# Splitting the queries' first weight pieces inside the keys-and-values stage, reloading the first pair's tokens there, and storing keys and values by two tiles

## What is computed

```
xn = layernorm(x);  ctx = ctx_2048
q = rope(rms_norm((xn @ wq).reshape(B, L, 16, 128), q_norm_w))
k = rope(rms_norm((xn @ wk).reshape(B, L, 4, 128), k_norm_w)); v = xn @ wv
k_ctx = rms_norm((ctx @ wk_ctx).reshape(B, T, 4, 128), k_norm_w); v_ctx = ctx @ wv_ctx
x = x + tanh(g_xattn[0]) * attend(q, [k_ctx, k], [v_ctx, v]) @ wo
```

## Time and profile before

| | |
|---|---|
| time, median of 3 runs | 2215.08 us (2214.99 to 2220.88) |
| the profiled execution's own time | 2212.68 us |
| its span (first to last instruction) | 2210.9 us |
| TensorE (PE) busy | 1969.8 us, 89% |
| VectorE (DVE) busy | 1369.9 us, 62% |
| ScalarE (ACT) busy | 1074.2 us, 49% |
| GpSimd (POOL) busy | 426.6 us, 19% |
| mean granted TensorE clock | 0.963 of full speed |

### The profile page before, as it was taken

The page is one execution under the profiler, slowest core; times in us unless marked ns, Lnnn a source line. Parts: engine busy times, 40 slices in busy tenths (PEclk is TensorE's granted clock), DMA queues, the critical chain, the costliest instruction groups (busy, mean ns, idle before and its releaser), DMA issues. The chain is left out here.

```text
span 2210.9 us, 33071 instructions
## 1 busy us (share of the span) xinstructions
PE 1969.8 (89%) x10514; PEld 1493.7 (68%) x10514; DVE 1369.9 (62%) x2405; ACT 1074.2 (49%) x2590; POOL 426.6 (19%) x512
## 2 busy tenths in 40 slices
PE   6999479999999999997998999999979988886898
PEld 5888357777666767765786777787768865554454
DVE  6777366766666676764321765645555436885786
ACT  3333156665655666663111622112324417995998
POOL 1111034444434444440000000000000001222111
PEclk9999789999999999998999999999989999998999
DMA  5665762233223241105442412113257623331121
GB/s 216 247 247 218 264 177 81 75 88 89 74 78 87 77 103 41 30 20 191 165 149 72 148 58 69 51 51 95 85 192 260 210 84 104 99 112 49 49 58 43
DMA packets 194087, 254.58 MB, mean 115 GB/s; under 512 B 11782, under 2 KB 144022, under 8 KB 183580
## 3 DMA queue, kind: packets, MB, share of 16 engines
q1 hardware_dynamic: 193948, 252.87, 35.1%
HBM read 152.14 MB, written 100.68 MB: 114 GB/s over the span
## 5 line engine op out<-in xcount | busy, mean ns | idle before, releaser
L937 ACT ACTIVATE at_prob<-at_S,at_bias,at_rq 128x384 f32<-128x384 f32 (+1 forms) x256 | 184.3, 731 | 166.0 <-DVE at_bias L1023 159.8
L1034 DVE TENSOR_TENSOR at_pt_lo<-at_PT,at_pt_hi 128x512 fp32r<-128x512 f32 x224 | 148.9, 689 | 92.5 <-ACT at_pt_hi L944 92.3
L805 POOL TENSOR_SCALAR at_prob<-at_prob,at_rsum 128x384 f32<-128x384 f32 (+1 forms) x256 | 161.2, 643 | 176.4 <-DVE at_rsum L1029 176.3
L864 PE MATMUL at_PT<-c_ident,at_prob 128*128 128x128 f32 x896 | 127.7, 277 | 44.1 <-DVE at_pt_lo L1034 44.1
L1604 ACT ACTIVATE gu_silu<-gu_G 128x512 f32<-128x512 f32 x64 | 38.1, 597 | 244.1 <-PE gu_G L103 234.7
L944 ACT ACTIVATE at_pt_hi<-at_PT 128x512 fp32r<-128x512 f32 x224 | 127.9, 603 | 54.2 <-PE at_PT L864 54.2
L1014 DVE TENSOR_REDUCE at_nmax<-at_S 128x1 f32<-128x384 f32 (+1 forms) x256 | 147.9, 616 | 7.0 <-PE at_S L857 6.6
L864 PEld LDWEIGHTS at_PT<-c_ident,at_prob 128*128 128x128 f32 x896 | 98.0, 140 | 75.0 <-DVE at_pt_lo L1034 70.5
L1642 DVE TENSOR_TENSOR gu_h<-gu_silu,gu_U 128x512 f32<-128x512 f32 x64 | 43.9, 686 | 143.9 <-PE gu_U L103 96.9
L853 PE MATMUL at_S<-at_k_hi,at_q_hi 128*128 128x384 f32 (+1 forms) x256 | 114.0, 445 | 16.9 <-DVE at_q_lo L1039 13.5
L796 POOL TENSOR_TENSOR at_rq<-at_qv,c_minus_half 128x4 f32<-128x4 f32 x64 | 65.2, 1019 | 287.2 <-DVE at_qv L1009 287.2
(11 more groups left out here) (308 smaller groups left out, 5485.3 us busy)
## 6 DMA issues: line engine op xcount, KB each, us to landing
wide<-at_ot SPq DMA_DIRECT2D x64, 256.0 KB, 2.8
wide<-gu_h SPq DMA_DIRECT2D x64, 256.0 KB, 3.2
o_a<-wide SPq DMA_DIRECT2D x14, 1024.0 KB, 4.8
d_a<-wide SPq DMA_DIRECT2D x13, 1024.0 KB, 8.6
keys_hi<-kv_kt_hi SPq DMA_DIRECT2D x8, 1024.0 KB, 4.0
keys_lo<-kv_kt_lo SPq DMA_DIRECT2D x8, 1024.0 KB, 6.0
values_hi<-kv_v_hi SPq DMA_DIRECT2D x8, 1024.0 KB, 8.0
values_lo<-kv_v_lo SPq DMA_DIRECT2D x8, 1024.0 KB, 9.6
```

Source lines behind the costliest of these rows:

```text
L805: pool.tensor_scalar(prob[u % 2][:, h, 0:n], prob[u % 2][:, h, 0:n], rsum[:, s:s + 1], 1.0, ALU.mult, ALU.mult).then_inc(normed.sem, 1)
L864: last = pe.transpose(bank_of("p", u, kb)[:, h * P:(h + 1) * P], prob[u % 2][:, h, kb * P:(kb + 1) * P], c.ident[:])
L937: act.activation(prob[u % 2][:, h, 0:n], S[h][:, 0:n], ACT.Exp, bias=bias[:, s:s + 1], scale=rq[u % 4][:, h:h + 1], accum_out=sums[:, s:s ...
L1034: dve.tensor_tensor(pt_lo[f % 4][:], bank_of("p", u, kb)[:], pt_hi[f % 4][:].bitcast(F32), ALU.subtract).then_inc(pt_done.sem, 1)
```

## The change

A new function reserves tiles that outlive stage 1: two of stage 1's weight rooms (high and low parts of pieces 0 and 1, the context's weights) and its context tokens `t_hi[1]`, `t_lo[1]` are now the same memory as stage 2's first two query weight pieces and its tokens of pair 0.

- In the last turn of stage 1, SP loads query pieces 0 and 1 into x and cx after the token stores; after the stores at n = 4 it loads both sequences' tokens of pair 0 back from memory.
- Keys and values are stored after every two tiles (n = 2, 4, 6, 8), in transfers of 512 KB instead of 1 MB. A key row of such a transfer is 1 KB long, where the whole tile was contiguous before.
- After the last unit, ACT copies the high parts and DVE subtracts the low parts of the two pieces; PE runs 24 keep-awake products.
- Stage 2 no longer loads or splits pieces 0 and 1, nor loads the tokens of pair 0; PE's keep-awake goes, and its wait for the tables stands after the projections of units 0 and 1. SP issues the four table loads first and then raises the tokens' semaphores itself.

```diff
 def keys_values(nc, io, c, scr):
+        c.make_queries(nc)
...
-        w_hi = [mem.sb(f"w_hi{i}", [P, DC, 512], F32R) for i in range(4)]
-        w_lo = [mem.sb(f"w_lo{i}", [P, DC, 512], F32R) for i in range(4)]
+        w_hi = c.wq_hi + [mem.sb(f"w_hi{i}", [P, DC, 512], F32R) for i in range(2, 4)]
+        w_lo = c.wq_lo + [mem.sb(f"w_lo{i}", [P, DC, 512], F32R) for i in range(2, 4)]
...
-        t_hi = [mem.sb(f"t_hi{s}", [P, DC, TOK], F32R) for s in range(SRC)]
-        t_lo = [mem.sb(f"t_lo{s}", [P, DC, TOK], F32R) for s in range(SRC)]
+        t_hi = [mem.sb("t_hi0", [P, DC, TOK], F32R), c.xt_hi]
+        t_lo = [mem.sb("t_lo0", [P, DC, TOK], F32R), c.xt_lo]
...
-                for n in (TT, 2 * TT):
-                    s, _ = source(n - 1)
+                if not more:
+                    sp.wait_ge(*ln.xn_ready.at(turn, TT))
+                    for i in range(2):
+                        sp.dma_start((x, cx)[i][:], wq[:, :, i * 512:(i + 1) * 512]).then_inc(wq_arrived[i], 16)
+                for n in (2, 4, 6, 8):
+                    s, t = source(n - 1)
+                    tok, tiles = slice((t - 1) * P, (t + 1) * P), slice(t - 1, t + 1)
                     wait_apart(sp, kt_done, turn, n, passed)
-                    sp.dma_start(scr.k_hi[turn, s], kt_hi[s][:]).then_inc(kv_stored[s].sem, 16)
-                    sp.dma_start(scr.k_lo[turn, s], kt_lo[s][:]).then_inc(kv_stored[s].sem, 16)
+                    for dram, keys in ((scr.k_hi, kt_hi), (scr.k_lo, kt_lo)):
+                        sp.dma_start(dram[turn, s, :, :, tok], keys[s][:, :, tok]).then_inc(kv_stored[s].sem, 16)
                     wait_apart(sp, v_done, turn, n, passed)
...
+                    for dram, values in ((scr.v_hi, v_hi), (scr.v_lo, v_lo)):
+                        sp.dma_start(dram[turn, s, :, tiles, :],
+                                     values[s][:, tiles, :].bitcast(F32)).then_inc(kv_stored[s].sem, 16)
                     if more and n == TT:
                         store_context(turn + 1)
+                    if not more and n == TT:
+                        sp.wait_ge(*xt_stored.at(0, 32))
+                        sp.wait_ge(*V_full.at(turn, TT))
+                        sp.dma_start(c.xt_hi[:].bitcast(F32), scr.xt_hi[0]).then_inc(queries_arrived, 16)
+                        sp.dma_start(c.xt_lo[:].bitcast(F32), scr.xt_lo[0]).then_inc(queries_arrived, 16)
...
+            sp.wait_ge(queries_arrived, 2 * 16)
             for s in (xt_stored, ct_stored, *kv_stored):
...
             turns(pe, body)
+            keep_awake(pe, T[0], c, 2 * AWAKE)
...
             turns(act, body)
+            for i in range(2):
+                act.wait_ge(wq_arrived[i], 16)
+                act.wait_ge(*V_full.at(PAIRS - 1, TT))
+                act.activation(c.wq_hi[i][:], (x, cx)[i][:], ACT.Copy).then_inc(wq_hi_done, 1)
...
             turns(dve, body)
+            for i in range(2):
+                dve.wait_ge(wq_hi_done, i + 1)
+                dve.tensor_tensor(c.wq_lo[i][:], (x, cx)[i][:], c.wq_hi[i][:].bitcast(F32),
+                                  ALU.subtract).then_inc(wq_lo_done, 1)
...
 def attention(nc, io, c, scr):
+        AHEAD = 2
...
-            weights.load(sp, 0)
-            load_xt(0, 0)
             sp.dma_start(cosw[:], io["c_cos_tok"]).then_inc(setup, 16)
             sp.dma_start(sinw[:], io["c_sin_tok"]).then_inc(setup, 16)
             sp.dma_start(qw[:], io["L0_xattn_q_norm_w"].partition_broadcast(P)).then_inc(setup, 16)
             sp.dma_start(mask_f[:], io["c_diag_mask"]).then_inc(setup, 16)
-            weights.load(sp, 1)
+            for b in range(2):
+                sp.sem_inc(xt_arrived[b].sem, 32)
             load_kv(0, 0, 0)
-            for n in range(2, HKV):
+            for n in range(HKV - AHEAD):
                 weights.load(sp, n)
-                load_kv(0, 0, n - 1)
-            load_kv(0, 0, HKV - 1)
-            load_xt(0, 1)
...
-            pe.wait_ge(weights.arrived[0], 16)
-            keep_awake(pe, O, c, AWAKE)
-            pe.wait_ge(tables, 3)
...
-                    pe.wait_ge(weights.ready, g + 1)
+                    if g >= AHEAD:
+                        pe.wait_ge(weights.ready, g + 1 - AHEAD)
...
             project(0, 1, 1)
+            pe.wait_ge(tables, 3)
             chain(pe, step)
...
-            weights.split_hi(act, 0)
             square(0, 0)
             keep_queries(0, 0)
             square(0, 1)
-            for i in range(1, HKV):
+            for i in range(HKV - AHEAD):
                 weights.split_hi(act, i)
...
-            weights.split_lo(dve, 0)
             rotate(0, 0)
             split_queries(0, 0)
             rotate(0, 1)
-            for i in range(1, HKV):
+            for i in range(HKV - AHEAD):
                 weights.split_lo(dve, i)
             chain(dve, step)
...
+    def make_queries(self, nc):
...
+        self.wq_hi = [far(f"wq_hi{i}", [P, DC, 512]) for i in range(2)]
+        self.wq_lo = [far(f"wq_lo{i}", [P, DC, 512]) for i in range(2)]
+        self.xt_hi = far("xt_hi", [P, DC, TOK])
+        self.xt_lo = far("xt_lo", [P, DC, TOK])
```

More of the change, by code:

```diff
@@ L265, in keys_values @@
     with ExitStack() as ctx:
+        c.make_queries(nc)
         mem = Alloc(ctx, nc, "kv_")
         SRC = 2
-        w_hi = [mem.sb(f"w_hi{i}", [P, DC, 512], F32R) for i in range(4)]
-        w_lo = [mem.sb(f"w_lo{i}", [P, DC, 512], F32R) for i in range(4)]
+        w_hi = c.wq_hi + [mem.sb(f"w_hi{i}", [P, DC, 512], F32R) for i in range(2, 4)]
+        w_lo = c.wq_lo + [mem.sb(f"w_lo{i}", [P, DC, 512], F32R) for i in range(2, 4)]
         wk, wv = [2, 0], [3, 1]
+        wq = io["L0_xattn_wq"].rearrange("(k p) n -> p k n", p=P)
         names = ["L0_xattn_wk_ctx", "L0_xattn_wv_ctx", "L0_xattn_wk", "L0_xattn_wv"]
@@ L320, in keys_values @@
         xt_stored = mem.counter("xt_stored", 32)
-        kv_stored = [mem.counter(f"kv_stored{s}", 64) for s in range(SRC)]
+        kv_stored = [mem.counter(f"kv_stored{s}", 128) for s in range(SRC)]
+        wq_arrived = [mem.sem(f"wq_arrived{i}") for i in range(2)]
+        wq_hi_done = mem.sem("wq_hi_done")
+        wq_lo_done = mem.sem("wq_lo_done")
+        queries_arrived = mem.sem("queries_arrived")
         first_setup = mem.sem("first_setup")
@@ L606, in _ @@
             turns(dve, body)
+            for i in range(2):
+                dve.wait_ge(wq_hi_done, i + 1)
+                dve.tensor_tensor(c.wq_lo[i][:], (x, cx)[i][:], c.wq_hi[i][:].bitcast(F32),
+                                  ALU.subtract).then_inc(wq_lo_done, 1)
 def attention(nc, io, c, scr):
     with ExitStack() as ctx:
+        ctx.enter_context(c.queries)
         mem = Alloc(ctx, nc, "at_")
@@ L619, in attention @@
         S_N = UNITS * GROUP
-        wq_hi = mem.sb("wq_hi", [P, DC, HQ * HD], F32R)
-        wq_lo = mem.sb("wq_lo", [P, DC, HQ * HD], F32R)
+        AHEAD = 2
+        wq_hi = c.wq_hi + [mem.sb(f"wq_hi{g}", [P, DC, GW], F32R) for g in range(AHEAD, HKV)]
+        wq_lo = c.wq_lo + [mem.sb(f"wq_lo{g}", [P, DC, GW], F32R) for g in range(AHEAD, HKV)]
         wq = io["L0_xattn_wq"].rearrange("(k p) n -> p k n", p=P)
-        xt_hi = [mem.sb(f"xt_hi{b}", [P, DC, L], F32R) for b in range(2)]
-        xt_lo = [mem.sb(f"xt_lo{b}", [P, DC, L], F32R) for b in range(2)]
+        xt_hi = [c.xt_hi[:, :, b * L:(b + 1) * L] for b in range(2)]
+        xt_lo = [c.xt_lo[:, :, b * L:(b + 1) * L] for b in range(2)]
         k_hi = mem.sb("k_hi", [P, HKV, 2, 2, L], F32R)
@@ L642, in attention @@
         prob = [mem.sb(f"prob{i}", [P, GROUP, 2 * L]) for i in range(2)]
-        weights = WeightSplit(mem, [(wq[:, :, g * GW:(g + 1) * GW], whole, wq_hi[:, :, g * GW:(g + 1) * GW],
-                                     wq_lo[:, :, g * GW:(g + 1) * GW]) for g in range(HKV)], raw=prob)
+        weights = WeightSplit(mem, [(wq[:, :, g * GW:(g + 1) * GW], whole, wq_hi[g][:], wq_lo[g][:])
+                                    for g in range(AHEAD, HKV)], raw=prob)
         pt_hi = [mem.sb(f"pt_hi{i}", [P, GROUP * P], F32R) for i in range(4)]
@@ L738, in load_xt @@
                 own = slice(b * L, (b + 1) * L)
-                sp.dma_start(xt_hi[b][:].bitcast(F32), scr.xt_hi[turn, :, :, own]).then_inc(xt_arrived[b].sem, 16)
-                sp.dma_start(xt_lo[b][:].bitcast(F32), scr.xt_lo[turn, :, :, own]).then_inc(xt_arrived[b].sem, 16)
+                sp.dma_start(xt_hi[b].bitcast(F32), scr.xt_hi[turn, :, :, own]).then_inc(xt_arrived[b].sem, 16)
+                sp.dma_start(xt_lo[b].bitcast(F32), scr.xt_lo[turn, :, :, own]).then_inc(xt_arrived[b].sem, 16)
             def load_kv(turn, b, g):
@@ L756, in _ @@
             sp.dma_start(mask_f[:], io["c_diag_mask"]).then_inc(setup, 16)
-            weights.load(sp, 1)
+            for b in range(2):
+                sp.sem_inc(xt_arrived[b].sem, 32)
             load_kv(0, 0, 0)
-            for n in range(2, HKV):
+            for n in range(HKV - AHEAD):
                 weights.load(sp, n)
```

(28 more changed lines are left out.)

2 lines of the change are left out of this document (removed).

## The result

The changed kernel takes 2191.98 us (median of 4 runs, 2189.59 to 2192.94) against 2217.98 us before (4 runs, 2214.99 to 2222.79); the ratio is 0.9879, 95% interval 0.9856 to 0.9903. The forecast was 2192.8 us, in a range of 2188 to 2200. As a difference it was 22.3 us; the two profiled executions, 2212.68 and 2191.29 us, differ by 21.4.

The account below looks back on a forecast made before the run. PE, busy 89% of the span, was taken as the bound, with some 64 us of handover holding 23 us of PE work. Gains of 4.4 + 11.8 + 6.1 = 22.3 us from 2215.08 gave 2192.8 us, range 2188 to 2200.

Parts of the forecast that it names:

- drain of stage 1: End of stage 1: half the bytes left to store, so the barrier comes 4.4 us earlier; bounds 0 to 5.5.
- head of stage 2, from there to PE's first projection: Start of stage 2: PE's first projection 2.3 us after the first load's issue instead of 14.1; gain 11.8 us.
- the clock in units 0 and 1: First projection of stage 2: as slow as now, at 1.2 GHz, no gain; bounds 1.7 us gained to 0.9 lost.
- the other two pieces: Stage 2's weight splits: only two pieces left, both with free rooms, so 6.1 us go.
- the 5.4 allowed: Head of stage 2: the mask's load may take 5.4 us to land without cost; upper bound of cost 1.7 us.
- the 0.9 allowed: Bound of the clock term: 0.9 us lost if all 12 matmuls of the first projection are slow.
- The drain shrank: Opposite of a rival at stage 1's end: drain does not shrink, gain 17.9 us, 2197.2 us; chance 0.14.
- new wait: Rival at stage 2's head: tables, first keys or pieces 2 and 3 late; 16.2 us left, 2198.9; chance 0.10.
- the clock did not hold: Opposite of a rival: clock holds through the barrier, drain ends with DVE; gain 25.1 us, 2190.0; chance 0.08.
- swallowed: Rival later in stage 2: something waited for at its own time swallows the gain, 2215 us; chance 0.04.
- The choking queue: Rival in stage 1's turns: key stores in 1 KB rows choke the queue, ending 0.3% slower; chance 0.02.

Follow-up runs that it names:

- stores by four: The changed kernel, but keys and values stored once per source in transfers of 1 MB, as before; ratio 0.9929, median 2199.4 us.
- the stores alone: The kernel before with only one part of the change, keys and values stored by two tiles; ratio 0.9984.
- one piece ahead: The changed kernel, but only the first weight piece is split ahead, leaving three for stage 2; ratio 0.9938.
- tokens first: The changed kernel, but SP raises the tokens' semaphores ahead of the four table loads instead of behind them; ratio 0.9902.
- e10_after_beside: The changed kernel unaltered, on the same chip and in the same rounds as the run with the splits in the stands; ratio 0.9905.

## Why the prediction was right

The forecast's own terms and what they measured, in the profiled executions:

| term | predicted, us | measured, us | from |
|---|---|---|---|
| drain of stage 1 | 4.4 | 4.1 | stage 2's start 251.49 to 247.40 |
| head of stage 2, from there to PE's first projection | 11.8 | 12.2 | 14.11 to 1.87 |
| the clock in units 0 and 1 | 0 (-0.9 to 1.7) | -1.2 | PE's start to the pair of subtractions: 17.85 to 19.02 |
| the other two pieces | 6.1 | 6.1 | pair of subtractions to maxima: 11.58 to 5.49 |
| sum | 22.3 | 21.3 | 300.32 to 279.06 |

*The drain.* The reason was right: half the bytes are left. The runs with stores by four and with the stores alone show it from both sides, 4.0 and 3.9 us. The last store landed at 245.1 where 244.8 was forecast. The rate of short rows was guessed at 331 GB/s from a mean; in the DMA view above the short key rows ran at 343 GB/s (mean of the ten slices from 347 to 351) and the long value rows at 409 (the ten behind them). DVE's two subtractions took 2.29 us each and ended at 243.2, so the stores ended last. Stage 2 started 2.3 us after the landing, as before.

*The head.* PE waited for SP's line L785, as said, for 1.87 us and not 2.3. The tables' last load landed 3.5 us after its issue, within the 5.4 allowed, and DVE waited for PE and ACT before it rotated. No keys and no weight piece were waited for.

*The clock.* This is the one term that left its bounds. The forecast had the level right (1.2 GHz at PE's start, and the 24 products worth nothing much), but put the first projection at its old speed and bounded nothing behind it. Eleven of its 12 matmuls were slow where about 8 had been, which cost 0.7 us of the 0.9 allowed (4.6 to 5.3 us up to ACT's first square); in the second projection, too, the clock rose later behind its start (4.0 us after it instead of 3.3), another 0.3 us that the forecast had not counted. Why the products did not help was shown by the windows: the clock fell at 243.9, PE started at 249.3. The Trainium skill ("TensorE: Matmul & The Clock Gate", Part 1) calls the throttled state the default that activity releases; the windows agree (0.50 while PE stood, 0.92 in the window from 254, five microseconds into its work).

*The pieces.* 6.1 us, and the run with one piece ahead gave 6.5 back.

*The rivals.* The drain shrank; there was no new wait; the clock did not hold; nothing was swallowed that the spread lets one see. The choking queue did not come: 1 KB rows cost more share per byte, 0.28 per 100 GB/s against 0.26, and that left PE alone.

The median of the kernel before moved up from 2215.08 to 2217.98 with a fourth run, so that the first ratio shows 26 us where profile and repeats show 21 to 23. That the time came out within 0.8 us of the forecast is therefore luck in part: the sum was 1.0 us too high, and the same kernel had medians of 2193.9 and 2195.1 us in its repeats.

## What to carry to other kernels

Between two stages look for what the barrier separates: bytes still to be stored when the last engine ends, and loads and preparations that wait for it only because their rooms lie behind it. Then ask which of the prepared pieces the next stage's chain really waits for, and in which engine's stand they would fit; here moving two splits and their loads by a few lines of program order brought DVE's maxima forward by another 5.6 us. Measure such a gain at a place in the trace just behind the handover, because the total of this kernel varies by several microseconds from stages that nobody touched.

## What the runs showed of the hardware that was not expected

- After the last matmul the clock stayed at 2.4 GHz for 1.8 us (before), for 2.3, 2.6 and 3.7 us (three executions of the changed kernel), for 4.1 us (tokens first, the same 24 products) and for 4.6 us (38 products: the last at 244.7, the fall at 249.3). The spread at 24 products reaches nearly to the value at 38, so the runs do not show that more products hold it longer. A stand of 4.66 us was passed at full clock, and the fall came as work began. So products close ahead of a stand may or may not carry the clock across.
- A load can land later than the bytes ahead of it explain: the first weight piece took 5.3 us with nothing issued before it and 7.7 us behind four loads of 384 KB in all, 2.4 us more, where 384 KB at the 298 GB/s of the earlier trace rows would take 1.3 (an estimate from that row).
- An issue on SP's queue took 0.34 to 0.43 us for the four small loads at the head of stage 2, except for one of them in three of the ten executions that issue them first: 1.56 us (stores by four) and 1.48 us (e10_after_beside) for the mask's, 1.57 us (tokens first) for the norm weight's. In the first two PE's start hung on it and came about 1.1 us later behind the start of stage 2. With the semaphores ahead of the issues PE started 0.12 us behind the start of stage 2 all the same.
